# Where U's bias is added for the twelve tiles mixed ahead of the experts: a second TensorE matmul in the mix, or VectorE on U's rows

## The reference, cut to what matters

```python
xn = layernorm(x)
q, k, v = (xn @ Wq + bq), (xn @ Wk + bk), (xn @ Wv + bv)   # 4 heads of 256 each
# every token attends over its own 4 heads only: a 4x4 softmax per token
scores = (einsum(q*cos, k*cos) + einsum(q*sin, k*sin)) / 16
out = swapaxes(softmax(scores) @ v, 1, 2).reshape(b, s, 4 * 256)
s = out @ Wo + bo
# 8 experts of width 512, the best 2 of each token by Sinkhorn gates
g = silu(xn + sum_top2(gate * (relu(xn @ wg) * (xn @ wp)) @ wo))
return x + s * g
```

## Time and profile before

| | |
|---|---|
| median of 3 runs | 1612.05 us (1609.37 to 1612.59) |
| span of the profiled execution, first to last instruction | 1604.5 us |
| TensorE matmul busy | 1536.4 us (96%) |
| TensorE weight load busy | 1169.5 us (73%) |
| VectorE busy | 974.2 us (61%) |
| ScalarE busy | 730.0 us (45%) |
| GpSimd busy | 794.2 us (49%) |
| granted TensorE clock, mean | 0.986 of full speed |

### The profile page before, as it was taken

One profiled execution on the slowest core, in us unless ns is written; L12 is line 12 of the kernel. 1 busy time (PEld: TensorE's weight loads), 2 busy tenths in 40 slices (PEclk: granted clock), 3 DMA queues, 4 the chain that ended last, 5 costly groups with the idle time before them and its releaser, 6 DMA issues.

```text
span 1604.5 us, 32706 instructions
## 1 busy us (share of the span) xinstructions
PE 1536.4 (96%) x11408; PEld 1169.5 (73%) x11408; DVE 974.2 (61%) x1880; ACT 730.0 (45%) x1205; POOL 794.2 (49%) x945
## 2 busy tenths in 40 slices
PE   5998899989999999999999999999999999999997
PEld 2545666668888888888888888866667766667773
DVE  7567989953333333333333333577888788888777
ACT  5775333413333333333333333545566565565552
POOL 4647588813333343433334433244565465844456
PEclk9999799989999999999999999999999999999999
DMA  9989842263223131222211141253565665455464
GB/s 328 396 331 323 297 157 90 71 253 143 89 99 132 54 132 54 98 87 94 88 57 54 57 158 57 86 172 134 172 202 172 217 211 185 160 169 176 153 211 145
DMA packets 162678, 251.22 MB, mean 157 GB/s; under 512 B 13928, under 2 KB 121248, under 8 KB 161376
## 3 DMA queue, kind: packets, MB, share of 16 engines
q1 hardware_dynamic: 147904, 211.47, 38.1%
q0 software_dynamic: 12960, 35.41, 6.6%
q10 hardware_dynamic: 1664, 2.26, 0.4%
HBM read 149.58 MB, written 99.50 MB: 155 GB/s over the span
## 4 chain that ended last, share of the span: by engine, by line
PE 88%; DVE 5%; DMA 4%; ACT 1%; issue 1%; POOL 0%; ACTq 0%; SPq 0%; DVEq 0%
PE ps L1143 21%; PE ps L1078 21%; PE ps L1089 13%; PE ps L1162 11%; PE ps L1025 7%; PE ps L1152 3%; DMA AUX<-xn_d,AUX 3%; PE ps L1046 2%; PE ps L1125 2%; PE ps L994 2%; PE ps L922 1%; PE ps L978 1%; PE ps L912 1%; DVE UN L1228 1%; DMA WR<-w_d 1%
## 5 line engine op out<-in xcount | busy, mean ns | idle before, releaser
L1143 PE MATMUL ps<-WR,FR 128*128 x1620 | 408.4, 401 | 5.7 <-issue 3.1
L1143 PEld LDWEIGHTS ps<-WR,FR 128*128 128x128 f32 x1620 | 296.6, 190 | 65.0 <-issue 7.6
L647 POOL DMA_INDIRECT y_d<-AUX x135 | 133.3, 987 | 366.8 <-ACT AUX L866 366.8
L1654 DVE TENSOR_TENSOR AUX<-AUX,ps 128x512 f32<-128x512 f32 x135 | 92.9, 688 | 347.3 <-ACT AUX L854 347.3
L815 ACT ACTIVATE WM<-ps,bcs,trig 128x512 f32<-128x512 f32 x256 | 252.1, 1016 | 89.8 <-PE ps L1078 83.0
L1594 DVE TENSOR_SCALAR WM<-ps,vec,trig 128x512 f32<-128x512 f32 x256 | 243.9, 993 | 62.3 <-ACT WM L815 61.6
L1089 PE MATMUL ps<-WM,XTJ 128*128 128x512 f32 x512 | 237.1, 600 | 0.0
L854 ACT ACTIVATE AUX<-ps 128x512 f32<-128x512 f32 x135 | 80.9, 599 | 323.7 <-PE ps L1143 323.7
L1078 PE MATMUL ps<-XH,WH 128*128 128x512 f32 x512 | 205.8, 402 | 4.9 <-issue 3.8
L1162 PE MATMUL ps<-WR,ABR 128*128 x1080 | 209.4, 292 | 0.0
L1078 PE MATMUL ps<-XH,WL 128*128 128x512 f32 x512 | 200.5, 392 | 0.0
(11 more groups left out here) (238 smaller groups left out, 2238.4 us busy)
## 6 DMA issues: line engine op xcount, KB each, us to landing
US<-u_d SPq DMA_DIRECT2D x63, 512.0 KB, 5.1
u_d<-UN SPq DMA_DIRECT2D x120, 256.0 KB, 2.0
WR<-w_d SPq DMA_DIRECT2D x8, 3072.0 KB, 10.8
AUX<-y_d SPq DMA_DIRECT2D x32, 512.0 KB, 5.5
WM<-in_L_attn_x_dram SPq DMA_DIRECT2D x16, 512.0 KB, 9.5
xn_d<-WM SPq DMA_DIRECT2D x32, 256.0 KB, 7.3
w_d<-USR SPq DMA_DIRECT2D x16, 512.0 KB, 4.5
AUX<-xn_d SPq DMA_DIRECT2D x16, 512.0 KB, 6.3
```

Source lines behind the costliest of these rows:

```text
L647: e.indirect_dma_start(y_d, bass.IndirectOffsetOnAxis(toks[:, m - 5:m - 4], 0), YS[:, (m - 5) % 2, :], None).then_inc(s_y[(m - 5) % 2], 16)
L1143: mm = e.matmul(b[:, :], x, WR[:, bass.ds(off[m] + (2048 * z + 1024 * a + 512 * k), 512)], start=(k == 0 and x is xh and z == 0), stop=(k ...
L1654: e.tensor_tensor(HS[:, m % 2, :], GR[:, :], mP[m % 2][:, :], ALU.mult).then_inc(s_h, 1)
```

## The change

For tiles 0 to 11 VectorE's `biased(n)` is left out and the mix gets a second matmul for each of the four slices, with the same 32 columns of `AT` and the constant row `BR` moving, added up in the same PSUM bank. A softmax row sums to one, so both give the same. The mix of these tiles waits for the load of `US` itself instead of for `biased`, and mix 0 for the load of `BR`.

```diff
+        def summed(n):
+
+            return n < 4 * QE - 4 or n >= 4 * NQ - 4
...
             def mix(n):
                 e.wait_ge(s_atc, n + 1)
-                if n < 4 * NQ - 4:
-                    e.wait_ge(s_ub, n + 1)
+                if n == 0:
+                    e.wait_ge(s_b3, 16 * 8)
+                if not summed(n):
+                    e.wait_ge(s_ub, n - 4 * QE + 5)
                 elif n == 4 * NQ - 1:
                     e.wait_ge(s_u63, 16)
                 else:
...
                 for c in range(4):
                     at = AT[:, n % 2, 32 * c:32 * c + 32]
-                    last = n < 4 * NQ - 4
+                    last = not summed(n)
                     mm = e.matmul(pM(n)[32 * c:32 * c + 32, :], at, us(n)[:, c, :], start=True, stop=last)
                     if not last:
                         mm = e.matmul(pM(n)[32 * c:32 * c + 32, :], at, BR[:, :], start=False, stop=True)
...
             def biased(n):
-                if n == 0:
+                if n == 4 * QE - 4:
                     e.wait_ge(s_b3, 16 * 8)
...
                                 spread(n + (c - 16) // 2)
-                                biased(n + (c - 16) // 2)
+                                if not summed(n + (c - 16) // 2):
+                                    biased(n + (c - 16) // 2)
```

## The result

| | us, median | runs | from | to |
|---|---|---|---|---|
| before | 1611.88 | 10 | 1604.61 | 1618.91 |
| with the change | 1619.95 | 10 | 1612.01 | 1623.70 |

The ratio is 1.0056 with a 95% interval of 1.0036 to 1.0076, so the change costs 9 us (5.8 to 12.3). The forecast was +4.2 us and 1616.2 us, with a range up to 1618.6. The sign was right, the size was not, and the time lies above the range.

What follows compares the result with a forecast made beforehand. TensorE was taken as the bound, with detours through VectorE and the store; mixes at 0.45 us gave shifts of 1.8, 2.85 and 4.2 us after quarters 1 to 3, so 1612.05 + 4.2 = 1616.2 us, range 1611.6 to 1618.6.

Steps and rivals of the forecast that it cites:

- What bounds it: From 204 to 332 us: TensorE's work, with detours through VectorE and the store of `RO` at quarter ends.
- VectorE's additions cost nothing to lose: Tiles 0 to 11: VectorE's 14.7 us saved turn into longer waits for the store, costed at 0.
- 0.45 us a mix: Each of the twelve mixes on TensorE gets 0.45 us longer from its four added matmuls; range 0.35 to 0.55.
- Slack of quarter 2: TensorE's 0.75 us wait for VectorE at quarter 2's end absorbs part of the mixes; shift there 2.85 us.
- wait of quarter 3: The fourth mix falls into TensorE's 4.42 us wait, leaving 3.97 us; the shift becomes 4.2 us.
- Rival 1, the clock stays up: From 336 us: the shorter TensorE idle time avoids the clock's fall, 2.3 us back, 1613.9 us; chance 0.14.
- Rival 2, the collision goes: At 233 to 239 us: GpSimd's `XTJ` 1.6 us earlier avoids VectorE's mark; 2.8 us back, 1613.4 us; chance 0.13.
- Rival 3, loads not overlapped: In the mixes: eight exposed weight loads make each 1.31 us longer, 13.7 us by quarter 3, 1625.7 us; chance 0.04.
- From 336 us on nothing is changed, so 4.2 us stay: From the experts on, the 4.2 us shift is handed on whole to the end.
- The range: Whole kernel: 1611.6 us, taking in the first two rivals, to 1618.6, a microsecond above twelve exposed mixes (1617.5).

Runs made afterwards that it cites:

- the control: The kernel before run once more with no edit: 1611.0 us over 12 runs, ratio 0.9996 (0.9979 to 1.0012).

## Why the prediction was wrong

- **What bounds it:** right. TensorE's own work from 204 to 332 us, and the detours through VectorE and the store, are in the chain after as before.
- **VectorE's additions cost nothing to lose:** right; 0.9994 without them, and the waits for the store grew.
- **0.45 us a mix:** right, 0.46. The stretches from a quarter's first U matmul to its scores grew by 1.4 to 1.8 us (19.91, 20.67 and 19.95 us against 18.44, 19.32 and 18.14 in the control).
- **Slack of quarter 2, wait of quarter 3:** sums right within 0.5 us. Quarter 3's wait came out to the hundredth, 3.98 for 3.97, and that is no luck of one trace: it is 4.4 us in the control, and 4.0 in the changed kernel with 64 and with 128 more. In quarter 2 TensorE still waited 0.57 us, not 0: its store took 3.53 us, with a packet inside.
- **Rival 1, the clock stays up:** it fell all the same, for 3.4 us:

```profile
341.50:344.90 3.40, 3.40 (x71) 3.40 (x68) 2.65 (x12) 0.36 (x3) 0.00 (x0) 0.50 1.15 489
```

- **Rival 2, the collision goes:** GpSimd's slowest mark fell from 2491 to 1434 ns, as its mechanism has it, but that gives TensorE nothing, and VectorE's collision comes and goes from one execution to the next (3476 ns before, 869 in the control, 4223 without the addition). The prediction's condition was also too easy: 1.6 us is how far GpSimd's `XTJ` starts ahead of the mark, but to be done by then it has to be 233.66 + 4.50 - 235.27 = 2.9 us earlier.
- **Rival 3, loads not overlapped:** refuted by the 1.02 us of a mix. Its 1625.7 us were nearer to some of the kernels above than my forecast, for another reason. The Trainium skill's rule behind it (TensorE: Matmul & The Clock Gate, Part 3: Packing small matmuls), that a weight load overlaps running matmuls only when its row group differs, does not hold for these four column groups.
- **The step that failed** is the sum's silent one: that added instructions cost what they take on their engine and nothing else. "From 336 us on nothing is changed, so 4.2 us stay" was wrong, because the change moves every packet of TensorE's instructions behind 207 us by 64, 128 and then 192 instructions. With the packets' ends put back from quarter 4 on, the kernel is +4.8 us by ratio (1.3 to 4.8 thousandths, that is 2 to 8 us), which the 4.2 fits. Without that it is +9, and its trace has stops at packets' seams of 2.54, 1.22 and 0.35 us, 4.1 in all, where before has 0.4.
- **The range** was too narrow for the same reason. Its upper end, 1618.6, allowed twelve exposed mixes and one microsecond of measurement, and nothing for packets; before's trace shows them arriving, but only one stop of 0.38 us. Idle instructions alone move this kernel by up to 13 us.

What stays open: why a packet starts 4.7 us behind TensorE's entry into the block at one seam, where the median is 1.0. The DMA engines are busy there (q1's packets take 60.5% of their time from 280 to 290 us), but they are in before too (60.3%), and no run changed that alone. Also open is why 64 and 128 idle instructions more lower the mean clock; in the trace of 128 more a fall follows a stop at once, but not every fall has a stop before it. And the stops don't account for all of every kernel's time: with 128 more on the changed kernel they add up to 1.4 us where the time without the clock's part is 8.0 us above before, 4.2 of it the mixes' by the sum. That packets and not some other effect of position make the stops rests on the period of 256 in the times and in the places of the 24 stops, on the time that always lies between a packet and its first instruction, and on the kernels with 128 and 256 more, which differ only by 128 idle instructions at the start. A kernel whose packets all come early was not tried.

## What to carry to other kernels

When TensorE is the bound and its instructions are many, an added or removed instruction shifts all code behind it against the packets it is fetched in. Before a difference of under 1% is put down to an edit, run the edit again with a whole packet's worth of instructions in all (idle ones in a pause make it up), or the kernel before with as many idle ones as the edit adds. If those move the time as much as the edit does, the edit isn't the cause. For a forecast, take the sum of durations as the middle and let the range reach as far as idle instructions could. Where 256 instructions pass in less than the time a packet needs, as in the scores here, look for a seam.

## What the runs showed of the hardware

- 64, 128 and 256 instructions without work, in a pause of TensorE, changed the time by +5, +13 and +2 us (the last with an interval of -2 to +5).
- TensorE's instructions arrive in packets of 256 while the kernel runs. Its first instruction behind a packet's seam never started less than 0.9 us behind the packet's end (1448 packets), and at the 24 stops 1.2 to 1.5 us behind it.
- A store of 128 KB in the chain takes 2.03 us, in seven of the eight undisturbed cases to the hundredth, and 2.8 to 4.3 us when a packet of instructions falls into it (eleven cases).
- A VectorE addition of 128x1024 that reads two tensors stretches a GpSimd mark beside it from 0.79 to 2.49 us. Without it the slowest is 1.43 to 1.48.
- The added half of a mix costs 0.46 us, where its eight matmuls' durations of 379 ns add up to 3.0 us and its eight weight loads' to 0.9: work on different column groups runs together.
- The same program's time varies from run to run by 10 us (control: 1605.7 to 1615.3 us over 12 runs), so that a pair of traces says little about 5 us.
